# Layer 1 of a two-layer block in two passes: attention rounds, then expert rounds

## Reference, cut to what matters

```
xn = _layernorm(x)
# gated linear attention: 4 heads, key width 32, value width 64, chunks of 64 tokens
q, k, v = xn @ Wq, xn @ Wk, xn @ Wv
gk = log_sigmoid(xn @ gk_w1 @ gk_w2 + gk_b2) / 16         # cumulated in a chunk: bi
qg, kg = q * exp(bi) * 32 ** -0.5, k * exp(-bi)
o = qg @ H + (qg @ kg.T * causal) @ v                      # H: the state, chunk by chunk
gla = (o / rms(o) * g_norm_w * g * sigmoid(g)) @ Wo        # g = xn @ Wg
# a transformer block: 16 heads of width 8
q, k, v = xn @ Wq + bq, xn @ Wk + bk, xn @ Wv + bv
probs = softmax(q @ k.T * 8 ** -0.5)                       # 512 x 512 for each head
y = _layer_norm(xn + (probs @ v) @ Wo + bo)
e = floor(y @ router_w + router_b) mod 4
ffn = _layer_norm(y + relu(y @ W1[e] + b1[e]) @ W2[e] + b2[e])   # 128 x 512 x 128
x = x + gla + ffn
```

## Time and profile before

| | |
|---|---|
| median of 2 runs | 3896.93 us (3894.93 to 3898.93) |
| span of the profiled execution | 3872.1 us |
| time of a run outside the span | 24.8 us |
| TensorE busy (PE) | 3095.8 us, 80% |
| VectorE busy (DVE) | 1983.7 us, 51% |
| ScalarE busy (ACT) | 1399.3 us, 36% |
| GpSimd busy (POOL) | 448.2 us, 12% |
| granted clock of TensorE, mean | 0.820 of full speed |

### The profile page before, as it was taken

How to read it: one execution, slowest core, us unless ns; L and a number is a source line. 1 busy time by engine, 2 the same in 40 slices (tenths; PEclk the granted TensorE clock), 3 DMA queues, 4 the chain that set the end, 5 groups by cost and what they waited for, 6 DMA issues and landing times.

```text
span 3872.1 us, 47514 instructions
## 1 busy us (share of the span) xinstructions
PE 3095.8 (80%) x16292; PEld 2116.7 (55%) x16292; DVE 1983.7 (51%) x3726; ACT 1399.3 (36%) x2025; POOL 448.2 (12%) x619
## 2 busy tenths in 40 slices
PE   5998899989899947778777787787687777877887
PEld 4777777777777733434444444445344444443454
...
PEclk9999999999999967777786786777777867767778
...
GB/s 71 6 6 5 11 5 5 5 5 10 6 5 5 5 69 16 18 33 10 24 34 7 27 24 17 27 18 17 33 7 27 34 7 27 18 18 33 18 17 7
DMA packets 61948, 71.40 MB, mean 18 GB/s; under 512 B 5564, under 2 KB 39376, under 8 KB 60880
## 3 DMA queue, kind: packets, MB, share of 16 engines
...
## 4 chain that ended last, share of the span: by engine, by line
PE 30%; DVE 12%; issue 6%; DMA 6%; ACT 5%; SPq 3%; POOL 2%; ACTq 0%; DVEq 0%; POOLq 0%
DVE b_row_max L1383 7%; PE b_psum L1161 7%; DMA b_k_stack<-qk_scratch 4%; PE b_psum L1108 4%; PE b_psum L1073 3%; PE b_psum L962 3%; SPq L917 3%; ACT b_prob L1239 3%; PE b_psum L1096 2%; PE b_psum L964 2%; PE b_psum L963 2%; PE b_psum L1041 1%; PE b_psum L1025 1%; DMA b_x<-x_scratch 1%; DVE b_acc L1465 1%
## 5 line engine op out<-in xcount | busy, mean ns | idle before, releaser
L1383 DVE TENSOR_REDUCE b_row_max<-b_psum 128x2 f32<-128x1024 f32 x512 | 592.3, 1218 | 145.3 <-PE b_psum L1073 144.8
L1239 ACT ACTIVATE b_prob<-b_psum 128x1024 f32<-128x1024 f32 x512 | 494.0, 1034 | 173.0 <-PE b_psum L1096 172.8
L1073 PE MATMUL b_psum<-b_k_stack,b_q_stack 24*128 24x512 f32 x1024 | 293.8, 719 | 259.8 <-DMA b_k_stack<-qk_scratch 143.8
L1260 ACT ACTIVATE b_hid<-b_psum,b_cols 128x512 f32<-128x512 f32 x256 | 176.0, 687 | 726.5 <-PE b_psum L964 726.4
L1073 PEld LDWEIGHTS b_psum<-b_k_stack,b_q_stack 24*128 24x128 f32 x1024 | 111.7, 259 | 439.5 <-DVE b_row_max L1383 267.2
L1108 PE MATMUL b_psum<-b_prob,b_v_aug 128*32 128x512 f32 x2048 | 320.2, 702 | 11.2 <-ACT b_prob L1239 10.9
L1096 PE MATMUL b_psum<-b_q_stack,b_k_stack 26*128 26x512 f32 x1024 | 216.4, 565 | 123.3 <-ACT b_prob L1239 80.0
L1161 PEld LDWEIGHTS b_psum<-b_w_plain,b_hid 128*128 128x128 f32 x2048 | 294.8, 229 | 19.5 <-ACT b_hid L1260 10.7
L1161 PE MATMUL b_psum<-b_w_plain,b_hid 128*128 128x128 f32 x2048 | 291.7, 311 | 5.9 <-ACT b_hid L1260 5.9
L1096 PEld LDWEIGHTS b_psum<-b_q_stack,b_k_stack 26*128 26x128 f32 x1024 | 86.3, 205 | 261.8 <-ACT b_prob L1239 186.3
L528 DVE SCALAR_TENSOR_TENSOR a_kv_sb<-a_psum,a_bias,a_v_sb 128x512 f32<-128x512 f32 x128 | 96.0, 750 | 221.9 <-ACT a_v_sb L446 221.9
...
## 6 DMA issues: line engine op xcount, KB each, us to landing
...
```

The source lines that it names most:

```text
L1073: mm = nc.tensor.matmul(psum[:, 2 + 2 * (i % 2) + x, :], q_stack[r, j, cut(t)], k_stack[r, j, :], start=True, stop=True)
L1239: nc.scalar.activation(prob[:, p % 4, :, :], psum[:, 2 + 2 * (p % 2):4 + 2 * (p % 2), :], ACT.Exp, scale=DH1 ** -0.5).then_inc(S["exp"], 1)
L1260: nc.scalar.activation(hid[:, i // HID % 2, i % HID, :], bank(f"w1{i}"), ACT.Relu, bias=col("b1", i)).then_inc(S["hid"], 1)
L1383: nc.vector.tensor_reduce(row_max[:, t, at:at + HPG + 1:HPG], psum[:, 2 + 2 * (i % 2):4 + 2 * (i % 2), :], AX.X, ALU.max).then_inc(S["row_ ...
```

## The change

Layer 1 no longer does a sequence in one round. `attention()` runs over all sequences first, then `experts()`; what the second needs (the normalised sum `xf` and the residual `r1`) goes through DRAM.

**The attention round.** `attention_order()` writes its order, one table for all engines. Each of the 32 pairs p of a round has first max p of the next sequence (stage B), then score p of this one (stage C), in even p the value product of the pair before (pv p/2 - 1), and then what a table puts there: the front of the sequence after the next (A0), the gated attention of the next (A1), the end of the one before (C2). Rounds at the ends leave out stages that have no sequence. Maxima use banks 4 and 5 alone, scores 2 and 3 alone, so the matmuls of pair p wait for the reader of pair p - 1. At p = 2, 10, 18, 26 the finished value sum is copied to `ao_sb`, and the transposes of it follow two pairs later.

**The stacks.** Maxima and scores have stacks of their own (`bq`, `bk` and `cq`, `ck`). 24 stores of 32 x 512 write a sequence's stacks to DRAM (`stack_scratch`) in their final layout, and each half of a stack pair (two of the four j) is loaded by 8 DMAs of 24 rows x 1024. The weights of q and k are permuted beforehand for that (`by_dim`), and their biases loaded by 16 small DMAs. The maxima come off in halves (mT 0 and 1), as a high row only (25 rows), straight from `m_sb` by DMA. The weights are prepared in four chunks instead of two.

**Smaller things.** v goes to `v_next` and is copied to `v_aug` on GpSimd in two halves; the block matrix of the states is made by one instruction. In `experts()` each w1 product stands behind the other without anything in between but the side work of the neighbouring sequences; y alternates between banks 0 and 1, the ring has the other six, and the loop does two sequences at a time.

```diff
--- before.py
+++ after.py
...
                 at = slice(first * P, (first + n) * P)
+                if first in by_dim:
+                    w = w.rearrange("p (g j d) -> p g d j", j=4, d=8)
...
 SPLIT_ROWS = 3 * DH1
-K_ROWS = SPLIT_ROWS + 2
...
+QK_ROWS = SPLIT_ROWS + 1
+OUT_OF = {"A0": 2, "A1": 1, "B": 1, "B2": 0, "C": 0, "C2": -1}
...
+    put(0, "A1", "gz")
+    put(0, "C2", "pv", STEPS - 1)
...
+    put(18, "B", "Cld", 0)
+    put(19, "A0", "mqklo")
+    put(19, "A1", "O", 0)
+    put(19, "B", "m_st", 0)
+    put(20, "A0", "qk_st")
...
+    order = []
+    for p in range(PAIRS):
+        order += [("B", "max", p), ("C", "score", p)]
+        if p >= 2 and p % 2 == 0:
+            order.append(("C", "pv", p // 2 - 1))
+        if p % 8 == 2 and p > 8:
+            order.append(("C", "ao", p // 8 - 1))
+        if p % 8 == 4 and p > 8:
+            order.append(("C", "aoT", p // 8 - 1))
+        order += at[p]
+    return order
+
...
+    for e in range(EXPERTS):
+        for m in range(HID):
+            order.append(("D", "w1", HID * e + m))
+            if m == 1 and e:
+                order.append(("D", "y", e - 1))
...
+        PV, SCORE, MAX, RING = 0, 2, 4, (1, 6, 7)
+        order = attention_order()
...
-            rounds(0, round_order)
-            with eng.Fori(1, BATCH - 1) as b:
-                rounds(b, round_order)
-            rounds(BATCH - 1, last_order)
+            for r in range(-2, 2):
+                rounds(0, r, live(r))
+            with eng.Fori(0, BATCH - 4) as b:
+                rounds(b, 2, order)
+            for r in range(BATCH - 2, BATCH + 1):
+                rounds(0, r, live(r))
 
         @block.sync
...
+                        until("qk_lo", stage, 2, 2)
+                        for w, parts in enumerate(((qk_hi, qk_hi, qk_lo), (qk_hi, qk_lo, qk_hi))):
+                            if w:
+                                until("max_filled", stage, PAIRS, -STEPS)
+                            for g in reversed(range(ROWG)):
+                                for c, src in enumerate(parts):
+                                    sp.dma_start(stacked(stage, w, 32 * g + DH1 * c, DH1).rearrange("d j s -> (d j) s"),
+                                                 src[32 * g:32 * g + 32, w, :].bitcast(F32)).then_inc(S["qk_st"], 16)
+                    elif kind == "Bld":
+                        if i == 0:
+                            until("qk_st", stage, 384, 384)
+                        else:
+                            until("max_filled", stage, PAIRS, 0)
+                        for w, dst in enumerate((bq, bk)):
+                            for g in reversed(range(ROWG)):
+                                src = stacked(stage, w, 32 * g, SPLIT_ROWS)[:, 2 * i:2 * i + 2, :]
+                                sp.dma_start(dst[32 * g:32 * g + SPLIT_ROWS, 2 * i:2 * i + 2, :].bitcast(F32),
...
+                        until("score_filled", stage, PAIRS, (i - 1) * STEPS)
+                        for w, dst in enumerate((cq, ck)):
+                            for g in reversed(range(ROWG)):
+                                src = stacked(stage, w, 32 * g, SPLIT_ROWS)[:, 2 * i:2 * i + 2, :]
+                                sp.dma_start(dst[32 * g:32 * g + SPLIT_ROWS, 2 * i:2 * i + 2, :].bitcast(F32),
+                                             src).then_inc(S[f"c_in{i}"], 16)
...
+                        until("m_neg", stage, 2, i + 1)
+                        for j in range(2):
+                            sp.dma_start(cq[SPLIT_ROWS:P:32, 2 * i + j, :].bitcast(F32),
+                                         m_sb[j:8:2, i, :].bitcast(F32)).then_inc(S[f"m_in{i}"], 16)
...
                     elif kind == "max":
...
-                        if i == 0:
-                            pe.wait_ge(S["stack_in"], 16 * 24 * n + 16 * 24)
-                        if i >= 2:
-                            pe.wait_ge(S["row_max"], MAXES * n + (i - 1))
-                        else:
-                            pe.wait_ge(S["exp"], MAXES * n)
-                        t, j, g2 = i // 8, i // 2 % 4, i % 2
+                        if i % STEPS == 0:
+                            until(f"b_in{i // STEPS}", stage, 128, 128)
+                        until("row_max", stage, PAIRS, i)
+                        j, t, g2 = i // 8, i // 2 % TILES, i % 2
                         for x in range(2):
-                            g = 2 * g2 + x
-                            r = slice(32 * g, 32 * g + SPLIT_ROWS)
-                            mm = nc.tensor.matmul(psum[:, 2 + 2 * (i % 2) + x, :], q_stack[r, j, cut(t)], k_stack[r, j, :],
-                                                  start=True, stop=True)
+                            r = slice(32 * (2 * g2 + x), 32 * (2 * g2 + x) + SPLIT_ROWS)
+                            mm = nc.tensor.matmul(psum[:, MAX + x, :], bq[r, j, cut(t)], bk[r, j, :], start=True, stop=True)
                         mm.then_inc(S["max_filled"], 1)
...
                     elif kind == "score":
...
-                            pe.wait_ge(S["mrow_in"], 32 * b + 32)
-                        j, kb = i // TILES, i % TILES
-                        for g2 in range(2):
-                            p = 2 * i + g2
...
-                            else:
-                                pe.wait_ge(S["row_max"], MAXES * b + MAXES)
-                            for x in range(2):
-                                g = 2 * g2 + x
-                                r = slice(32 * g, 32 * g + K_ROWS)
...
-                            mm.then_inc(S["score_filled"], 1)
...
+                            until(f"c_in{i // STEPS}", stage, 128, 128)
+                            until(f"m_in{i // STEPS}", stage, 32, 32)
+                        until("exp", stage, PAIRS, i)
+                        j, kb, g2 = i // 8, i // 2 % TILES, i % 2
+                        for x in range(2):
+                            r = slice(32 * (2 * g2 + x), 32 * (2 * g2 + x) + QK_ROWS)
+                            mm = nc.tensor.matmul(psum[:, SCORE + x, :], ck[r, j, cut(kb)], cq[r, j, :], start=True, stop=True)
+                        mm.then_inc(S["score_filled"], 1)
                     elif kind == "pv":
                         j, kb = i // TILES, i % TILES
-                        pe.wait_ge(S["exp"], MAXES * b + (2 * i + 2))
...
+                        if i % 8 == 0:
+                            until("vcopy", stage, 2, i // 8 + 1)
+                        if kb == 0:
+                            until("ao_ready", stage, HPG, j)
                         for g in range(ROWG):
-                            mm = nc.tensor.matmul(psum[32 * g:32 * g + 32, 0, :], v_aug[:, kb, HPG * j + g, :],
+                            mm = nc.tensor.matmul(psum[32 * g:32 * g + 32, PV, :], v_aug[:, kb, HPG * j + g, :],
                                                   prob[:, (2 * i + g // 2) % 4, g % 2, :],
...
                     elif kind == "score":
...
-                            p = 2 * i + g2
-                            act.wait_ge(S["score_filled"], MAXES * b + (p + 1))
-                            if p >= 4:
-                                act.wait_ge(S["pv_done"], STEPS * b + (i - 1))
-                            elif p == 0:
-                                act.wait_ge(S["pv_done"], STEPS * b)
-                            nc.scalar.activation(prob[:, p % 4, :, :], psum[:, 2 + 2 * (p % 2):4 + 2 * (p % 2), :], ACT.Exp,
-                                                 scale=DH1 ** -0.5).then_inc(S["exp"], 1)
...
-                                act.wait_ge(S["own_filled"], n_own(b, f"aoT{j - 2}"))
-                            nc.scalar.copy(ao_sb[:, j % 2, :], psum[:, 0, :]).then_inc(S["ao_ready"], 1)
+                        until("score_filled", stage, PAIRS, i + 1)
+                        until("pv_done", stage, STEPS, i // 2 - 1)
+                        nc.scalar.activation(prob[:, i % 4, :, :], psum[:, SCORE:SCORE + 2, :], ACT.Exp,
+                                             scale=DH1 ** -0.5).then_inc(S["exp"], 1)
+                    elif kind == "ao":
+                        until("pv_done", stage, STEPS, TILES * (i + 1))
...
+                        nc.scalar.copy(ao_sb[:, i % 2, :], psum[:, PV, :]).then_inc(S["ao_ready"], 1)
...
                     elif kind == "max":
-                        t, j, g2 = i // 8, i // 2 % 4, i % 2
-                        dve.wait_ge(S["max_filled"], MAXES * n + (i + 1))
-                        at = HPG * 2 * g2 + j
-                        nc.vector.tensor_reduce(row_max[:, t, at:at + HPG + 1:HPG], psum[:, 2 + 2 * (i % 2):4 + 2 * (i % 2), :], AX.X,
+                        j, t, g2 = i // 8, i // 2 % TILES, i % 2
+                        until("max_filled", stage, PAIRS, i + 1)
+                        at = 8 * (j // 2) + 4 * g2 + j % 2
+                        nc.vector.tensor_reduce(row_max[:, t, at:at + 3:2], psum[:, MAX:MAX + 2, :], AX.X,
```

(15 more changed lines are left out.)

1215 lines of the change are left out of this document (706 added, 509 removed), and 6 rows, old and new, of the table FREE.

## The result

The changed kernel takes **3791.65 us** (median of 2 runs, 3790.15 to 3793.16), 0.973 of the kernel before (95% interval 0.970 to 0.976). It is faster, as forecast, and inside the range, but 105 us faster where 301 were forecast. By the spans it is less still: 3872.1 to 3791.3 us, 81 us. The 24.8 us that the prediction put on top of a span were not a fixed cost: the changed kernel's profiled run lies 1.9 us above its span, and so does every later run of the kernel before (1.8 us), so the profiled execution of the earlier trace rows was a faster one than the two of the median. The ratio of the runs is what counts.

What follows compares the result with a forecast made beforehand. The prediction took TensorE at a low clock in one half of the round, and joints between halves, as the bound. 15 x 100 + 215 + 16 x 28 = 2163, with setup 2173 for 2474.5, gave 3596 us, range 3400 to 3800.

Steps and rivals of the forecast that it cites:

- clock term of T: Attention round: time lost when TensorE drops to 1.2 GHz in half-empty pairs; 7 us, bounds 0 and 32.
- T: Length of one full attention round of 32 pairs, 15 such rounds; forecast 100 us.
- copy waits: Attention round, pairs 2, 10, 18, 26: value product waits for the copy to ao_sb; 1.8 us x 4 = 7 us.
- sum of 93: Attention round at full clock: 58 link, 17 TensorE side work, 7 copy, 3 ScalarE at pair 0, 8 VectorE side work.
- rival 2: Attention round at 1.2 GHz throughout, each matmul group waiting for its only buffer: 125 us, 3996 us total; chance 0.10 with in-between.
- Link: Attention round: each max waits for the reduce of the one before, 1.81 us a pair, 32 x 1.81 = 58 us.
- Experts round: Experts pass, nothing woven in, dense at 2.4 GHz: 28 us a round, bounds 28 and 36.
- rival 4: Experts pass not dense: 36 us a round, +128 us, 3724 us; chance 0.20 together with rival 3.
- Stack loads: Attention round: chain from stores to the next first max, 23 us, hidden; it replaces the 9.6 us stall.
- rival 3: Attention round: stack loads bind or over half VectorE's side work exposed; T 108 to 116, chance 0.20 together with rival 4.
- Ends and setup: Incomplete attention rounds, the joint between passes and the experts' end 215 us, plus 10 us setup before layer 1.
- VectorE's exposed side work: Attention round: part of VectorE's some 24 us of side work that isn't hidden; 8 us, bounds 0 and 24.

Runs made afterwards that it cites:

- e6: Changed kernel with value-sum copy a pair earlier, two side-work banks, 82 unread matmuls a round (4 in bare pairs, 2 in others, 8 ahead of score 1): 3473.77 us.
- e1: Changed kernel with the copy of a finished value sum one pair earlier (pairs 1, 9, 17, 25): 3669.49 us, ratio 0.946.
- e8: Changed kernel with the early copy, three double banks in turn for maxima and scores, side work on bank 1 alone: 3995.53 us, ratio 1.028.
- e11: Changed kernel with the early copy, side work on bank 1 alone, maxima and scores keeping their banks, 6 and 7 unused: 4060.26 us, ratio 1.041.

## Why the prediction fell short, step by step

**The step that failed is the clock term of T**: "Bounds of the clock term: 0, and 32 us ... I take 7 us". T was forecast at 100 us and is 112.2. The sum without the clock was 93 us, 86 without the copy waits; e6, without these waits and at a clock of 1.00, takes 92.15 us with 82 fillers in it, so the sum of 86 is at most 6 us too low. The clock term isn't 7 us but at least 104.9 - 92.15 = 12.7, and about 19 if the sum of 93 was right (112.2 - 93). Of the 12.2 us by which T was missed, 5.7 are the clock's by this floor; the other 6.5 are the clock's too or an error in the sum of 86, which no run tells apart. Over 15 rounds T accounts for some 180 of the 220 us by which the span of 3571 was missed.

The reason given for a small term failed too: "a drop there makes TensorE fuller until it rises again". In the trace above TensorE was fuller, 27.6 of 30.8 us, and the clock stayed at 1.2 GHz for all of them.

What led the step astray was the choice of rows. It weighed the row of the last scores and the 38.8 us of the side-loaded stretch, both at 1.00, against the row at 0.66, and took the value near them. But in both TensorE was busy for 87 to 94% of the time, with two double banks in turn. The prediction had itself worked out that at the high clock TensorE has 59 us of work in 93, and a stretch with so many holes was in none of the rows at 1.00. In the changed kernel even the round that has scores and value products but no maxima, close to the work of the earlier trace rows, ran cold with one double bank:

```profile
3222.00:3310.00 88.00, 63.22 (x232) 17.75 (x230) 5.25 (x22) 35.74 (x38) 4.47 (x5) 0.52 0.05 14
```

The busy share that TensorE shows at 1.2 GHz hides the holes: 100.65 of 115.80 us in the slow round above. The 59 us themselves are too low: they count 64 groups of two matmuls at 0.22 us, where the prediction's own pairs have 0.43, and with that it is 72. From e6 I estimate 69: 88.3 us busy a round at 1.00, less 82 fillers at the 0.24 of the earlier trace rows. The holes are then 24 us in 93 rather than 34, and the clock fell all the same. By the same slip the bound of 125 us for a round at 1.2 GHz throughout, twice the 59 and the copy waits, is too low. (The side work was also shared out as 11.3 and 15.1 us, 26.4 of its 28.5; with all of it, T moves by 2 us at most.)

Of the rival readings, rival 2 and the rule put beside it were nearest in mechanism. The Trainium skill, page "TensorE: Matmul & The Clock Gate", section "A second HAM failure mode: psum-queue depth-cycling", says that small idle gaps between matmul groups that step through PSUM banks make the clock go back and forth. The trace agrees: 0.60 and 0.69 in the two rounds above, 0.50 and 1.00 within one, and 1.00 in e6, where the gaps hold work.

The other terms of the sum:

- **Link**: reduces of the changed kernel in bare pairs were to be 1.8 to 2.1 us apart. Two in a row at 2.4 GHz are 1.81 us apart, two at 1.2 GHz 2.12 us:

```profile
2340.09 1.23 DVE L1364 TENSOR_REDUCE c_row_max<-b_psum 128x2 f32<-128x1024 f32 x1 [1.03 <-PE b_psum L1106]
...
2341.90 1.23 DVE L1364 TENSOR_REDUCE c_row_max<-b_psum 128x2 f32<-128x1024 f32 x1 [0.59 <-PE b_psum L1106]
...
2421.11 1.22 DVE L1364 TENSOR_REDUCE c_row_max<-b_psum 128x2 f32<-128x1024 f32 x1 [0.60 <-PE b_psum L1106]
...
2423.23 1.22 DVE L1364 TENSOR_REDUCE c_row_max<-b_psum 128x2 f32<-128x1024 f32 x1 [0.89 <-PE b_psum L1106]
```

- **Copy waits**: 7 us a round forecast, 6.6 in the trace, 7.4 back in e1. Right.
- **Experts round**: 28 us forecast, 27.1 measured, clock 1.00. Right; rival 4 (36 us) is out.
- **Stack loads**: forecast hidden, and hidden in every round, where they had cost 9.6 us. The 20.7 us that TensorE waits for them are one wait, ahead of the first maxima of all. The chain of rival 3 is out; T came out in its span of 108 to 116 us, but not by that chain. Its other half, VectorE's side work exposed to more than half, is spoken of below.
- **Ends and setup**: 225 us forecast; 3791.3 - 1397.6 - 15 x 112.2 - 16 x 27.1 = 277 measured. The setup accounts for 16.2 instead of 10: the first load of x starts at 1413.80 for 1397.58.

```profile
1413.80 0.44 SPq L931 DMA_DIRECT2D c_x<-x_scratch  x1
```

  The end of the experts takes 28 instead of 10: from their first product at 3329.3 to the end of the span at 3791.3 it is 462.0 us, 16 x 27.1 and 28.4. The other 27 us lie in the rounds at the ends of the attention pass, as the one at a clock of 0.52 above, and in those four of the 15 full rounds that are outside the window of 11.

The sum of the misses: 15 x 12.2 + 52 - 14 = 221 us, the 220 us of the span. **Rival 2**, cold throughout at T = 125, was put at 0.10 with the gaps as its mechanism; the mechanism was the right one, it acted by half, and e8 and e11 show its full form at 128 and 131 us a round.

**VectorE's exposed side work** (8 us) wasn't measured by itself. With e6 at most 6 us above the sum, it is 14 us or less of its 24 if the other terms hold, so that the second half of rival 3 isn't ruled out by itself. How the 92 us of e6 divide into link, side work and fillers stays open, and so does what a round at full clock without fillers would take: no kernel here kept the clock without them.
